# Two layers of attention and feed-forward on one core: value products in pairs with eight probability buffers, and another order in the second QKV stage

## What is computed

```python
x = x + 0.5 * _L0_ffn_ref(_layernorm(x, axis=-1), ...)     # linear map with a low-rank addition
x = x + _L0_attn_ref(_layernorm(x, axis=-1), ...)          # 32 heads of 16, 8 key heads, rotary, causal
x = x + 0.5 * _L0_ffn_ref(_layernorm(x, axis=-1), ...)
x = x + 0.5 * _L1_ffn_ref(_layernorm(x, axis=-1), ...)     # linear map and top-2 of 8 low-rank experts
x = x + _L1_attn_ref(_layernorm(x, axis=-1), ...)          # 8 heads of 32, causal
x = x + 0.5 * _L1_ffn_ref(_layernorm(x, axis=-1), ...)
```

## Time and profile before

| | us |
|---|---|
| runs | 1273.25, 1272.96, 1280.2 |
| median | 1273.25 |
| profiled execution: its own time | 1285.09 |
| profiled execution: span from first to last instruction | 1283.3 |
| mean granted TensorE clock in it | 0.929 of full speed |

### The profile page before, as it was taken

The page is one execution under the profiler, slowest core; times in us unless marked ns, Lnnn a source line. Parts: engine busy times, 40 slices in busy tenths (PEclk is TensorE's granted clock), DMA queues, the critical chain, the costliest instruction groups (busy, mean ns, idle before and its releaser), DMA issues.

```text
span 1283.3 us, 21563 instructions
## 1 busy us (share of the span) xinstructions
PE 1192.6 (93%) x6800; PEld 744.0 (58%) x6800; DVE 915.8 (71%) x2958; ACT 661.6 (52%) x1015; POOL 396.2 (31%) x521
## 2 busy tenths in 40 slices
PE   4999999999889998999989999999998999989988
PEld 1775443444358997545878644443332889855478
DVE  5778897999527868663777798998880578676365
ACT  1732574666545644444545136666666356445542
POOL 1433431221144520115624434122123445002261
PEclk9897696999899999899999958998897999989999
DMA  9555221131001014100241742112200100430001
GB/s 301 189 147 125 84 76 26 27 78 50 2 1 52 2 34 99 60 2 1 83 166 40 194 122 76 27 27 60 68 3 1 34 19 1 99 92 2 1 10 58
DMA packets 40053, 81.44 MB, mean 63 GB/s; under 512 B 6044, under 2 KB 7580, under 8 KB 39532
## 3 DMA queue, kind: packets, MB, share of 16 engines
q1 hardware_dynamic: 39944, 80.06, 21.8%
HBM read 50.02 MB, written 28.13 MB: 61 GB/s over the span
## 4 chain that ended last, share of the span: by engine, by line
PE 71%; DVE 14%; issue 5%; DMA 4%; ACT 3%; POOL 2%; SPq 1%; DVEq 0%; ACTq 0%; POOLq 0%
PE bank L1060 17%; PE bank L927 12%; PE bank L833 6%; PE bank L835 6%; PE bank L834 6%; PE bank L1041 5%; DVE maxes L1280 5%; PE bank L819 3%; DVE unused L1276 3%; PE bank L1035 3%; PE bank L937 2%; DVE features L1209 2%; PE bank L858 2%; PE bank L909 1%; PE bank L860 1%
## 5 line engine op out<-in xcount | busy, mean ns | idle before, releaser
L1528 ACT ACTIVATE probs<-bank 128x1024 f32<-128x1024 f32 (+3 forms) x416 | 366.0, 911 | 278.3 <-PE bank L1041 195.4
L927 PE MATMUL bank<-ops 48*128 48x512 f32 (+3 forms) x960 | 315.3, 432 | 10.5 <-DVE maxes L1280 3.4
L1276 DVE CUSTOM_DVE_ANT_0 unused<-bank,causal 128x128 bf16<-128x128 f32 (+3 forms) x640 | 279.1, 486 | 44.7 <-PE bank L927 40.7
L1660 POOL TENSOR_SCALAR_AFFINE_SELECT probs<-probs 128x256 f32<-128x256 f32 (+1 forms) x256 | 119.4, 467 | 575.5 <-ACT probs L1528 574.5
L927 PEld LDWEIGHTS bank<-ops 48*128 48x128 f32 (+1 forms) x960 | 160.6, 205 | 194.3 <-DVE maxes L1276 77.3
L1060 PE MATMUL bank<-probs,v_mem 128*17 128x512 f32 (+6 forms) x1920 | 256.2, 542 | 1.4 <-ACT heads_raw L1515 0.8
L1280 DVE TENSOR_REDUCE maxes<-bank 128x1 f32<-128x512 f32 x320 | 207.2, 684 | 50.3 <-PE bank L927 49.3
L1041 PE MATMUL bank<-ops 50*128 50x512 f32 (+2 forms) x640 | 181.7, 464 | 8.0 <-DMA ops<-shiftT 4.6
L1041 PEld LDWEIGHTS bank<-ops 50*128 50x128 f32 x640 | 89.9, 205 | 68.0 <-issue 35.4
L833 PE MATMUL bank<-ops,xT 128*128 128x512 f32 (+1 forms) x288 | 114.0, 396 | 6.7 <-DVE xT L1119 2.6
L1119 DVE TENSOR_TENSOR xT<-bank,xT 128x512 fp32r<-128x512 f32 (+1 forms) x96 | 61.5, 644 | 75.5 <-ACT xT L1390 75.4
(11 more groups left out here) (128 smaller groups left out, 1903.8 us busy)
## 6 DMA issues: line engine op xcount, KB each, us to landing
query_rows_dram<-ops SPq DMA_DIRECT2D x48, 256.0 KB, 4.3
ops<-query_rows_dram SPq DMA_DIRECT2D x64, 192.0 KB, 4.4
w_odd<-staging_wqkv SPq DMA_DIRECT2D x4, 1536.0 KB, 6.8
x<-x_dram SPq DMA_DIRECT2D x16, 256.0 KB, 4.1
ops<-features SPq DMA_DIRECT2D x64, 64.0 KB, 2.0
ops<-ops SPq DMA_DIRECT2D x16, 256.0 KB, 3.0
out_dram<-x SPq DMA_DIRECT2D x16, 256.0 KB, 2.0
staging_wqkv<-wqkv_dram SPq DMA_DIRECT2D x2, 1536.0 KB, 14.2
```

The lines of the kernel that those rows point to most:

```text
L927: last = mm(dst[:, h * w:(h + 1) * w], queries(a, u)[rows, t // 4, hi, t % 4 * P:(t % 4 + 1) * P], keys(a, u, hi)[rows, HALF * kp:HALF * k ...
L1276: V.tensor_tensor_reduce(unused[:, masked % 3, 0:w], part, causal[:, HALF - w:], 1.0, NEG, ALU.add, ALU.max, dst).then_inc(s["max_done"].s ...
L1528: A.activation(probs[:, e % 6, :, 0:cols], scores[:, 2 * (e % 2):2 * (e % 2) + 2, 0:cols], ACT.Exp, scale=a.scale).then_inc(s["exp"].sem, 1)
L1660: G.affine_select(out=p, in_=p, compare_op=ALU.is_ge, fill=0.0, base=0, pattern=pattern, channel_multiplier=-1).then_inc(s["masked"].sem, 1)
```

## The change

Three things are changed.

1. `probs` has 8 buffers in place of 6, and the exponential of event e waits for the values of event e-8.
2. The loop of both attentions takes the values of two steps on end: at g with (g - lag) odd it does `value(g-lag-1)` and `value(g-lag)`. For A0 (lag 2) that is at every odd g, with none at even g; A1 (lag 3) stays at even g. `plan_ring` and its slots are the same.
3. In the second QKV stage block (3,0) comes before the first values, the values of tokens 0 to 3 are split into two pairs that stand ahead of block (0,1) and behind block (3,1), and 22 ring items of unit 0, not 21, are done inside the stage, in ticks 6 to 10. On SP the shift rows of unit 0 for c=1 come ahead of the rows of block (2,0).

```diff
-            order = [(0, 0), (1, 0), first, (3, 0), (0, 1), (1, 1), (3, 1), second, (2, 1), (2, 0)]
-            self.ring_in = {4: (0, 0, 1, 1), 5: (1, 1, 1, 1), 7: (0, 0, 1, 1), 8: (1, 2, 2, 2), 9: (1, 2, 2, 1)}
+            order = [(0, 0), (1, 0), (3, 0), first[:2], (0, 1), (1, 1), (3, 1), first[2:], second, (2, 1), (2, 0)]
+            self.ring_in = {6: (1, 1, 1, 1), 7: (1, 1), 8: (1, 1, 1, 1), 9: (1, 2, 2, 2), 10: (1, 2, 2, 0)}
...
+PROBS = 8
...
-        probs = sb("probs", [P, 6, 2, HALF])
+        probs = sb("probs", [P, PROBS, 2, HALF])
...
-                for j, g in ((0, 0), (1, 0), (3, 0), (0, 1), (1, 1), (3, 1)):
+                for _, j, g in [p for p in A1.products if p[0] == "qk" and p[1] != 2]:
                     rows_of_block(b, j, g)
                 load_shifts(b, QKV1, 0, 0)
-                for j, g in ((2, 1), (2, 0)):
-                    rows_of_block(b, j, g)
+                rows_of_block(b, 2, 1)
                 load_shifts(b, QKV1, 0, 1)
+                rows_of_block(b, 2, 0)
...
-                                  v[:, j, a.kv_head(u, r, i), :], probs[:, e % 6, n, first:first + w],
+                                  v[:, j, a.kv_head(u, r, i), :], probs[:, e % PROBS, n, first:first + w],
...
-                    if a.row_tiles == 2:
-                        if a.lag <= g < a.units * ns + a.lag:
-                            value(g - a.lag)
-                    elif g % 2 == 0 and g > a.lag and g - a.lag < a.units * ns:
+                    if (g - a.lag) % 2 == 1 and g > a.lag and g - a.lag < a.units * ns:
                         value(g - a.lag - 1)
                         value(g - a.lag)
...
-                            if e >= 6:
-
-                                act.wait_ge(s["pv"].sem, s["pv"].at(b, a.step_of(e - 6) + 1))
+                            if e >= PROBS:
+
+                                act.wait_ge(s["pv"].sem, s["pv"].at(b, a.step_of(e - PROBS) + 1))
```

More of the change, by code:

```diff
@@ L1524, in attention @@
                             act.wait_ge(s["scored"].sem, s["scored"].at(b, e + 1))
-                            if e >= 6:
-                                act.wait_ge(s["pv"].sem, s["pv"].at(b, a.step_of(e - 6) + 1))
-                            A.activation(probs[:, e % 6, :, 0:cols], scores[:, 2 * (e % 2):2 * (e % 2) + 2, 0:cols],
+                            if e >= PROBS:
+                                act.wait_ge(s["pv"].sem, s["pv"].at(b, a.step_of(e - PROBS) + 1))
+                            A.activation(probs[:, e % PROBS, :, 0:cols], scores[:, 2 * (e % 2):2 * (e % 2) + 2, 0:cols],
                                          ACT.Exp, scale=a.scale).then_inc(s["exp"].sem, 1)
@@ L1654, in attention @@
                         pool.wait_ge(s["exp"].sem, s["exp"].at(b, e + 1))
-                        p = probs[:, e % 6, :, 0:cols].rearrange("p n (i q) -> p n i q", q=w)[:, :, :, 0:P]
+                        p = probs[:, e % PROBS, :, 0:cols].rearrange("p n (i q) -> p n i q", q=w)[:, :, :, 0:P]
                         pattern = [[0, 2], [0, cols // w], [1, P]] if cols > w else [[0, 2], [1, P]]
                         if cols == w:
-                            p = probs[:, e % 6, :, 0:P]
+                            p = probs[:, e % PROBS, :, 0:P]
                         G.affine_select(out=p, in_=p, compare_op=ALU.is_ge, fill=0.0, base=0,
```

## The result

The changed kernel takes 1369.24 us (median of 4 runs, 1364.46 to 1370.64) against 1273.11 for the kernel before (4 runs, 1267.1 to 1280.2). The ratio is 1.0746, 95% interval 1.0685 to 1.0808: 7.5% slower, 96 us. The forecast had the sign and missed the size: 1297, range to 1335.

The account below looks back on a forecast made before the run. In A0 VectorE, 93% busy, was taken as the bound, its idle time lengthening units one for one. Terms +26 + 6 - 3 - 5 = +24 on 1273.25 gave 1297 us; range 1258 to 1335, ends of the sum 1252 and 1359.

Parts of the forecast that it names:

- The units at full clock: A0 units at full clock: pairs make VectorE idle longer, +2.2 us a unit over 28.2, +26 us in all.
- The third and fourth gap: VectorE's idle times behind a unit's two 512, 512 pairs in A0: from 0.31 to 1.17 and 0.17 to 1.03 us.
- the first: A0 unit's first pair (512, 384): VectorE's idle time behind it grows from 0.65 to 1.51 us, taken as 1.4.
- the fifth: A0 unit's fifth pair (512, 384): starves nobody, since VectorE's arithmetic for a finished shift stands ahead of it.
- the 12.0 units of the forecast: A0 time at full clock in both batches: 11.2 units in units 1 to 6 plus 0.8 from unit 0.
- The faster rival: A0: pairs save TensorE's changes of kind, 1.9 us a unit, if VectorE still has work; 1242 us, chance 0.15.
- The clock: Units 1 to 6 of A0: time at half clock rises from 43 to 60 us, at 0.37 us each, +6 us.
- The rival: Clock rival: thinner stretches between A0's pairs bring half clock to half of the time, +51 us; 1342 us, chance 0.20.
- At half clock nothing is added: A0 at half clock: a pair costs what two single value steps cost, 1.47 us of VectorE idle time each; +0.
- The last unit: Last unit of A0, without maxima: pairs halve ScalarE's waits for scores, -3 us for both batches.
- Eight buffers: Eight buffers of probs: waiting for the values of event e-8 costs nothing.
- The second QKV stage: Second QKV stage: three TensorE waits (0.78, 2.12, 1.48 us) shrink, 2.5 us a batch, -5 us in all.

Follow-up runs that it names:

- e2: The changed kernel, pairs kept, with each score of A0 issued twice (640 matmuls more): 1291.89 us, ratio 1.0177 to the kernel before.
- e7: The changed kernel, pairs kept, with A0's scores issued twice only at even steps, those without values: 1325.38 us, ratio 1.0392 to the kernel before.
- e8: The changed kernel, pairs kept, with A0's scores issued twice in units 0 to 6 and once in unit 7: 1291.16 us, measured once.
- e1: The changed kernel with A0's values taken singly again; eight buffers and new QKV order stay: 1269.18 us, ratio 0.9989 to the kernel before.
- e9: e1 with the ring's maximum matmuls issued twice in the first three steps of A0: 1274.88 us, ratio 1.0022 to the kernel before.
- e3: The changed kernel, pairs kept, with the ring's maximum matmuls of A0 issued twice, scores once: 1351.54 us, ratio 1.0647 to the kernel before.

## Why the prediction was right and wrong, step by step

**The units at full clock: right in sum, in part by luck.** The forecast was 30 to 31 us and +2.2 a unit; e2, e7 and e8 show 30.4. The third and fourth gap came as worked out (1.17 and 1.04 for 1.17 and 1.03). The other pairs did not: behind the first stood 0.55 us and not 1.4, behind the fifth, which was to starve nobody, 0.67, and behind the sixth, a short one, 0.22. These errors cancel: the five gaps of e2's unit sum to 3.65, where 3.60 was forecast. VectorE's idle time is 30.4 - 26.49 = 3.9 us a unit, where 1.94 + 2.16 = 4.1 was forecast. Since those units issue some scores twice, the pairs' own share lies between 1.2 and 2.2 us a unit, 14 to 26 us over the 12.0 units of the forecast.

**The faster rival: its condition isn't met.** It needed VectorE without idle time, and 3.9 us of idle time a unit stayed. The Trainium skill, TensorEngine Tiling (Array Packing), Key Properties, has the drain at a change of tiling mode; it may well be saved six times a unit, but no run here shows a unit with pairs that is shorter for it.

**The clock: the step that failed.** "... so I take a little more half clock, 60 us: +6 us." Measured were 218 us in units 1 to 6, 175 more than the 43 of before; at 0.31 us each that is an estimate of 54 us in place of 6. The spans agree with it: units 1 to 6 grew by 76.9 us, of which the pairs at full clock (1.2 to 2.2 us in each of the forecast's 11.2 units there) make an estimated 13 to 25, which leaves 52 to 64. The step argued that a unit is 8% longer and thins out a little, and moved the 43 us by 17; no row gave that size. It took the time at half clock for something that shifts a little, where it grew fivefold. The rival had it: "If the thinner stretches between pairs bring it down in every unit, to half of the time". 218 of the 436.7 us are half of the time, and its price, 51, is close to the 54: its time (180 us) was too short, and its 0.37 for each is above the 0.31. It got a chance of 0.20 and its 1342 lay outside the range that was given; even the outer end of the sum, 1359, lay below what was measured. What it left out is small: against the kernel before, unit 7 grew by 4.7 and 3.0 us, and unit 0 by 1.9 and 1.5 (46.5 and 48.8 before, batch 1 not shown).

What TensorE did before one of the falls shows in the windows of the values' line alone (L1061; length, busy PE and PEld, clock, DMA share, GB/s) in the changed kernel, where the clock falls from 1.00 to 0.50 at 330.0:

```profile
325.20:330.00 4.80, 0.00 (x1) 0.00 (x0) 1.00 0.00 1
```

and in e2, between the same two pairs of a unit, where it stays at 1.00:

```profile
263.60:268.80 5.20, 0.00 (x0) 0.00 (x0) 1.00 0.02 4
```

Pairing took the values out of every second step, and in both kernels there is a stretch with none, filled by ring matmuls and scores. With the scores issued once the clock fell at its end; with the scores issued twice it did not. But this fall is not like all: ahead of the other 13 in units 1 to 6 of batch 0, a stretch as long held 0.2 to 1.9 us of values. That the pairs brought the clock down is shown by e1, and that more score matmuls bring it back by e2 (0.99 and 1.00) and in part by e7. Which property of the work between pairs decides is not shown.

The Trainium skill, TensorE: Matmul & The Clock Gate, A second HAM failure mode: psum-queue depth-cycling, describes a kernel whose engine idles shortly and often between groups of matmuls while it cycles through PSUM banks, and whose clock swings between its two levels by that. The ring of three banks is such a place: in the changed kernel's unit from 235.00, at a clock of 0.68, the list of waits has TensorE's loads for the ring waiting for VectorE often and shortly (us in total, times, longest).

```profile
PEld bank L928 <- DVE maxes L1274: 3.7, 12, 0.5
```

But the trace of the kernel before has such waits as well, 4.7 us in 10 at a clock of 1.00; so waits of this kind don't by themselves tell the two apart. The section What's actually happening of the same page of the Trainium skill was named for this rival in the forecast: by it, throttled is the default and activity lifts it. e2's 77 us agree with that; e9, with more matmuls and a lower clock, does not.

**At half clock nothing is added: right in kind.** 2.90 us behind a pair, against 2 x 1.47.

**The last unit: wrong in sign.** -3 was forecast, since pairs would halve ScalarE's waits for scores. The same list of waits in the changed kernel, over unit 7 of batch 0 (us in total, times, longest):

```profile
ACT probs L1526 <- PE bank L1042: 11.6, 5, 3.2
```

There were 5 waits where 6 had been, not half as many, and they took 11.6 us in place of 6.1. The unit grew by 4.7 us in batch 0, where its clock went from 0.90 to 0.75, and by 3.0 in batch 1, where it went from 0.73 to 0.70. At 1.00 the pairs gained nothing either: 22.7, with some scores twice, against 21.3.

**Eight buffers: right**, as far as single values show it: in e1 a unit at full clock takes 28.3 us (not shown), as before. With pairs it wasn't measured apart.

**The second QKV stage: right in size, not in its parts.** A1's first unit is 22.3 and 22.2 us, as against 24.5 in both batches of the kernel before (not shown); -2.2 and -2.3 for the -2.5 forecast. The timeline of the changed kernel, with the lines that answer to the earlier trace rows:

```profile
551.39 0.28 PE L933 MATMUL bank<-identf,shifts 128*16 128x128 f32 x1 [0.35 <-DVE maxes L1274]
...
553.61 0.97 PE L928 MATMUL bank<-ops 96*128 96x384 f32 x2 [1.54 <-DVE maxes L1274]
...
553.95 0.27 DVE L1287 COPY shiftT<-bank 16x128 f32<-16x128 f32 x1
...
554.25 1.38 SPq L653 DMA_DIRECT2D ops<-shiftT  x2
...
556.79 1.22 PE L1036 MATMUL bank<-ops 98*128 98x512 f32 x2 [1.55 <-DMA ops<-shiftT]
```

The 0.78 us wait for the rows of block (1,1) is gone, but the stage ahead of A1 is as long as before (142.8 and 143.1 us for 143.0 and 142.9, not shown), with one more ring item in it. The wait for the shift transpose went from 2.12 to 0.35 us, more than the 0.8 taken, but most of it only moved: the ring matmul behind the transpose now waits 1.54 us for VectorE, where no wait stood before. Together 0.2 us is gained. The shift's DMA is issued 0.03 us after VectorE is done (553.95 + 0.27 = 554.22), as forecast; but the score's wait for it is 1.55, where 1.48 was before. From the end of VectorE's copy to the score it is 2.57 us in place of 3.32, 0.75 less where 0.6 was forecast; the wait is no shorter because TensorE itself came to it sooner. In the median nothing of this can be told: e1 has the same stage and measures 0.9989 with an interval of 0.6% around it.

## What to carry to other kernels

Before work is bunched, ask what is left in the stretches it leaves, and in what state TensorE's clock will be there: a clock that is already seen to fall now and then (twice in six like units here) may fall far more often (14 times), and the price is then that of half the stage and not of a few per cent more of it. Price the change at both levels from rows; where no row says at which level the changed stage will run, let the range reach to the price at the lower one. A share of busy time won't show it (93% before and after); the granted clock by stretch does, and issuing some harmless matmuls twice is a cheap experiment that tells a clock from a queue (e2), if they don't stand in the queue themselves (e3).

## What the runs showed of the hardware

Issuing 640 matmuls more, without use, made the kernel 77 us faster (1369.24 to 1291.89). Not every added matmul came with a higher clock: in unit 0 of batch 0, with pairs, 39 more scores came with 0.75 (e2), 76 more of the ring's matmuls with 0.63 (e3), and none with 0.61. A us at half clock cost this kernel 0.29 to 0.40 us, as read from e2, from e7 and from executions of the kernel before. And the clock can fall in units of one and the same program (e7, 1.00 and 0.80 side by side), so one unit's length says little; it takes all of a stage's units to see which level holds.
